# Layer 3's attention with a new order of heads, value products in four column groups, row sums by matmuls with ones, and the division behind the product

## The chip, the cores and the metric

The kernel runs on one core of one Trainium2 chip. The metric is the device time of one execution, in microseconds (us). TensorE (PE) multiplies, VectorE (DVE), ScalarE (ACT) and GpSimd (POOL) work elementwise, SyncE (SP) issues DMAs. "PEld" in the profile is TensorE loading weights, which can lie beside its matmuls.

## What is computed

The program is a chain of four layers; the change is in the last, a cross-attention in which four query heads share a key and value head. Cut to what matters:

```python
B, L, S, H, NH, KVH, HD, GROUPS = 8, 100, 361, 512, 32, 8, 16, 4
q = hidden @ Wq + bq;  k = enc @ Wk + bk;  v = enc @ Wv + bv      # hidden (8,100,512), enc (8,361,512)
q = q.reshape(b, l, KVH, GROUPS, HD).transpose(0, 2, 3, 1, 4)      # k, v: (b, KVH, s, HD)
scores = einsum('bkgld,bksd->bkgls', q, k) / sqrt(HD) + mask
attn = softmax(scores, axis=-1)
out = einsum('bkgls,bksd->bkgld', attn, v).transpose(0, 3, 1, 2, 4).reshape(b, l, H)
x = layernorm(out @ Wo + bo + hidden) * gamma + beta
```

So there are 8 batches of 32 heads, 256 heads in all, each with 100 queries against 361 keys (padded to 363 = 3 x 121).

## The kernel before

`layer3` runs three phases: `layer3_queries`, `layer3_attention` and `layer3_output`. Only the second changes, and with it the order in which the third loads the rows of Wo.

Work goes head by head, and the order on each engine is written out by hand. TensorE takes a "step" for each head h: `scores` (L2252) multiplies the queries of head h with the keys of its pair (96 rows, 364 columns, in the one-pass float32 format) into one of two PSUM banks; `turn` (L2259) transposes the probabilities of head h-4 in three pieces of 121 keys; `attend` (L2272) makes, on three of every four steps, one float32 product of values and turned probabilities of one key and value head. The four heads g of a value head lie side by side in 400 columns; three products (one for each piece j of 121 keys) run over the keys. The output has 32 rows, since the values of an even head fill rows 0 to 15 and those of an odd head rows 16 to 31, with zeros in the other half, so that the two heads of a pair m accumulate in one bank, which is one of two. From step 16 of each batch on, the keys of the next batch (L2230, four products) and its values (L2239, twelve) are projected, a product or four at the end of a step.

VectorE adds the mask, negates and takes the row minimum in one custom instruction (L2402, followed by a read of the accumulator), which frees the bank of the scores; then it inverts the row sum of head h-2 (L2396) and scales that head's probabilities in place (L2407). At the end of a pair it copies four blocks of the product to `attT` (L2385). ScalarE takes the exponential with the row sum beside it (L2326, with a read of the accumulator), and copies the turned probabilities out of PSUM to `probsT` (L2333). GpSimd adds the two parts of the context of the next batch but one (L2202) and spreads the queries over heads (L2211, twelve instructions a batch), once `scored` tells that the scores of the batch two back are done.

TensorE's scores of head h wait for `shifted` of h-2 (two banks), its transposes for `scaled` and for `turned_copied` of two heads back, its value products for `turned_copied` of the fourth head. The lines:

```python
for step in range(H3 + (TAIL if last else 0)):
    if step < H3: scores(step)
    if step - TURN < H3 and not (first and step < TURN): turn(step - TURN)
    v, j = divmod(step - ATTEND - Q3 + 1, Q3)
    if j < NT3 and not (first and v < 0): attend(v, j)
```

## Time and profile before

| what | us |
|---|---|
| median of 3 runs | 4331.4 |
| lowest and highest run | 4328.82, 4335.36 |
| span of the profiled execution | 4338.2 |
| of it, the layer 3 attention from its first scores to its last copy (3736.5 to 4278.6) | 542.1 |
| busy in the whole span: PE, DVE, ACT, POOL | 3694.2, 1757.5, 1221.5, 559.9 |

The profile is of one execution, with a span 6.8 us above the median. A row of the timeline gives start, length, engine, line, operation, output and inputs, the shape and the number of instructions merged; in brackets stands how long the engine had been idle and what ended it. The length of a matmul is its own latency, and matmuls overlap: what one costs in a row of them is the distance from its start to the next start. A float32 product is recorded as two matmuls (x2). The granted clock ("PEclk") is the share of 2.4 GHz; 0.50 is 1.2 GHz.

### The profile page before, as it was taken

How to read it: one execution, taken by the hardware profiler on the slowest of the kernel's cores; microseconds unless marked ns; L12 is line 12 of the kernel's file. 1: busy time of each engine (PE TensorE's matmuls, PEld its weight loads, DVE VectorE, ACT ScalarE, POOL GpSimd, SP SyncE). 2: the span in 40 equal slices, each digit the busy share in tenths (PEclk: the TensorE clock that was granted, in tenths of full speed). 3: DMA queues.
4: the chain of work that ended last, by engine and by line, in shares of the span. 5: the costliest groups of instructions: out<-in, count | busy, mean ns of one | idle time of the engine just before them, and what ended most of it. 6: DMA issues, size and time to landing. Idle time of an engine off the chain costs nothing. (4 is left out here: it accounts for less than half of the span.)

```text
span 4338.2 us, 51209 instructions
## 1 busy us (share of the span) xinstructions
PE 3694.2 (85%) x17671; PEld 2781.4 (64%) x17671; DVE 1757.5 (41%) x3586; ACT 1221.5 (28%) x3084; POOL 559.9 (13%) x475
## 2 busy tenths in 40 slices
PE   4999979796658699999989789898989979688886
PEld 3777758453324487887878578787878867344442
DVE  2445442318873423323232422323232241566664
ACT  2344332111011123222222222222222232445452
POOL 0000020123430300000000100000000010432312
PEclk9999989899979799999999899999999989768688
DMA  2110120100000312222121132222122120110001
GB/s 85 48 46 25 37 77 15 38 10 3 0 10 29 106 42 78 74 59 80 41 73 46 38 109 55 84 55 84 41 78 55 27 80 10 61 38 27 31 2 31
DMA packets 142038, 209.09 MB, mean 48 GB/s; under 512 B 18915, under 2 KB 104357, under 8 KB 141933
## 3 DMA queue, kind: packets, MB, share of 16 engines
q0 software_dynamic: 67584, 94.64, 8.5%
q1 hardware_dynamic: 74348, 113.17, 8.5%
q8 instruction: 51, 0.84, 0.1%
q14 instruction: 55, 0.44, 0.0%
HBM read 191.04 MB, written 13.47 MB: 47 GB/s over the span
## 5 line engine op out<-in xcount | busy, mean ns | idle before, releaser
L63 PE MATMUL work<-cT_layer_hi,wk_layer_hi 128*128 128x362 f32 x1024 | 390.3, 381 | 0.0
L1908 ACT ACTIVATE p_layer<-scores,neg_max_layer 100x362 f32<-100x362 f32 x256 | 144.5, 565 | 740.4 <-DVE neg_max_layer L1963 739.1
L1944 DVE TENSOR_TENSOR values_layer<-work,value_bias_layer 121x512 f32<-121x512 f32 x192 | 132.4, 690 | 519.3 <-PE work L65 519.3
L64 PE MATMUL work<-cT_layer_lo,wk_layer_hi 128*128 128x362 f32 x1024 | 336.8, 329 | 0.0
L65 PE MATMUL work<-cT_layer_hi,wk_layer_lo 128*128 128x362 f32 x1024 | 336.6, 329 | 0.0
L63 PE MATMUL work<-wv_layer_hi,cT_layer_hi 128*121 128x512 f32 x768 | 311.9, 406 | 0.0
L64 PE MATMUL work<-wv_layer_lo,cT_layer_hi 128*121 128x512 f32 x768 | 303.1, 395 | 0.0
L65 PE MATMUL work<-wv_layer_hi,cT_layer_lo 128*121 128x512 f32 x768 | 302.6, 394 | 0.0
L1751 POOL DMA_DIRECT2D cT_layer_hi<-ctxT_hi x64 | 47.7, 745 | 1745.5 <-PE work L65 1743.3
L1890 ACT ACTIVATE keysT_layer<-work 128x361 f32<-128x361 f32 x256 | 120.7, 472 | 510.4 <-PE work L65 510.4
L1820 PE MATMUL o<-pT_layer,values_layer 121*128 121x100 f32 x1536 | 215.8, 276 | 56.9 <-ACT pT_layer L1914 56.9
L1820 PEld LDWEIGHTS o<-pT_layer,values_layer 121*128 121x128 f32 x1536 | 205.4, 191 | 87.5 <-ACT pT_layer L1914 70.2
L2272 PE MATMUL att<-probsT,values 121*32 121x400 f32 x384 | 217.9, 659 | 43.8 <-ACT probsT L2333 43.8
L1963 DVE TENSOR_REDUCE neg_max_layer<-scores 100x1 f32<-100x362 f32 x256 | 136.3, 532 | 220.5 <-PE scores L1802 220.4
L2326 ACT ACTIVATE probs<-probs,neg_max 100x363 f32<-100x363 f32 x256 | 152.6, 596 | 248.0 <-DVE neg_max L2402 246.9
L63 PEld LDWEIGHTS work<-cT_layer_hi,wk_layer_hi 128*128 128x128 f32 x1024 | 193.9, 189 | 29.1
L64 PEld LDWEIGHTS work<-cT_layer_lo,wk_layer_hi 128*128 128x128 f32 x1024 | 194.3, 190 | 24.3
L2402 DVE CUSTOM_DVE_ANT_0 probs<-scores,mask 100x363 f32<-100x363 f32 x256 | 134.8, 527 | 172.5 <-PE scores L2252 171.2
L1802 PE MATMUL scores<-keysT_layer,qT_layer 128*100 128x362 f32 x512 | 198.7, 469 | 0.0
L65 PEld LDWEIGHTS work<-cT_layer_hi,wk_layer_lo 128*128 128x128 f32 x1024 | 193.5, 189 | 0.0
L63 PE MATMUL work<-l_hT_hi,wq_layer_hi 128*128 x256 | 101.8, 398 | 97.1 <-DVE qT_layer L1955 54.6
L2211 POOL TENSOR_TENSOR q_heads<-q_batch,head_rows 32x800 fp32r<-32x800 f32 x96 | 146.0, 1521 | 279.6 <-PE scores L2252 272.2
(353 smaller groups left out, 7737.9 us busy)
## 6 DMA issues: line engine op xcount, KB each, us to landing
cT_layer_hi<-ctxT_hi POOLq DMA_DIRECT2D x64, 722.0 KB, 4.9
cT_layer_lo<-ctxT_lo POOLq DMA_DIRECT2D x64, 722.0 KB, 6.1
l0mlp_staged<-in_L_xattn_mlp_w_dram SPq DMA_DIRECT2D x16, 512.0 KB, 4.2
staged_layer<-in_L_xattn_wq_dram SPq DMA_DIRECT2D x8, 1024.0 KB, 5.2
staged_layer<-in_L_xattn_wk_dram SPq DMA_DIRECT2D x8, 1024.0 KB, 5.1
staged_layer<-in_L_xattn_wv_dram SPq DMA_DIRECT2D x8, 1024.0 KB, 5.1
staged_layer<-in_L_xattn_wo_dram SPq DMA_DIRECT2D x8, 1024.0 KB, 5.6
l2mlp_staged<-in_L_xattn_w_fc_dram SPq DMA_DIRECT2D x16, 512.0 KB, 4.1
```

Of the source, the lines that this page charges most:

```text
L63: pe.matmul(out, cut_a(a.hi), cut_b(b.hi), start=start, stop=False)
L64: pe.matmul(out, cut_a(a.hi), cut_b(b.lo), start=False, stop=False)
L65: return pe.matmul(out, cut_a(a.lo), cut_b(b.hi), start=False, stop=stop)
L1802: pe.matmul(ps_scores[x % 2][0:L, 0:KEYS2], qT[:, j, c * L:(c + 1) * L], keysT[c % 2][:, j, :], start=True, stop=True).then_inc(scored, 1)
L1820: mm = pe.matmul(ps_o[:, j * L:(j + 1) * L], values[c % 2][:, n, j * P:(j + 1) * P], probsT[x % 2][:, n, :], start=(n == 0), stop=(n == NT ...
L1908: act.activation(probs[x % 4][:, 0:KEYS2], ps_scores[x % 2][0:L, 0:KEYS2], ACT.Exp, bias=neg_max[:, x:x + 1], accum_out=sums[:, x:x + 1]). ...
L1944: dve.tensor_tensor(values[c % 2][:, j, :], bank("v", c, j)[0:T2, :], value_bias[:, min(j, 1), :], ALU.add).then_inc(dve_copied, 1)
L1963: dve.tensor_reduce(neg_max[:, x:x + 1], ps_scores[x % 2][0:L, 0:KEYS2], AX.X, ALU.max, negate=True).then_inc(maxed, 1)
L2211: pool.tensor_tensor(q_heads[s][R * block_:R * (block_ + 1), 2 * m:2 * m + 2], q_batch[s][rows, part].unsqueeze(1).broadcast_to([R, 2, Q3, ...
L2272: mm = pe.matmul(ps_att[m % 2][0:R, 0:Q3 * L], values[slot(s, v)][:, j, m, e, :], probsT[v % 2][:, j, :], start=(e == 0 and j == 0), stop= ...
L2326: act.activation(probs[h % PROBS][:], probs[h % PROBS][:], ACT.Exp, bias=neg_max[:, h:h + 1], scale=-1.0, accum_out=sums[:, h:h + 1]).then ...
L2402: dve.tensor_tensor_reduce(probs[h % PROBS][:], ps_scores[h % 2][0:L, 0:N3], mask_add[s][:], -1.0, 3e38, ALU.add, ALU.min, neg_max[:, h:h + 1]
```

## The change

- The heads of a batch are taken in another order (`head_of`): first the 16 heads of the four even value heads (e = 0, pairs m = 0 to 3, four heads g each), then the 16 of the odd ones.
- Turned probabilities of 16 heads are kept (`probsT` has two sets of four tiles). The value products of such a group stand together in three steps, j = 0, 1, 2, of 16: in each, four products for the pairs m, whose outputs are the rows 32m to 32m+31 of one PSUM bank, and behind them four products of the same probabilities with a constant `ones` (1 in the 16 columns of parity e), which write the row sums, 16 times over, in the same places of a second bank.
- The exponential has no accumulator any more; the inverse and the scaling for each head go. Once a batch, VectorE inverts the sums (128x400) and multiplies the product with them into `attT` (128x4x100), in place of 16 small copies.
- The copies of the turned probabilities are shared: ScalarE takes even heads, VectorE odd ones. The transposes now stand 3 steps behind the scores, not 4.
- Loops are written out in full; the four `memset`s of `ones` and other semaphores come with it. Rows of Wo are loaded in eight DMAs as before, in the order that fits the new `attT`.

```diff
-    SCALE, TURN, ATTEND = 2, 4, 5
-    TAIL = ATTEND + NT3 - 1 + 1
-    NEXT = 16
+    GROUP = PAIRS * Q3
+    HEADS = B * H3
+    TURN = 3
+    BURST = GROUP + TURN + 1
+    NEXT = GROUP
+
+    def head_of(h):
+
+        b, x = divmod(h, H3)
+        e, x = divmod(x, GROUP)
+        m, g = divmod(x, Q3)
+        return b, e, m, g
...
+        ones = sb("ones3", [T3, 2, R])
...
-        probsT = [sb(f"probsT3_{i}", [T3, NT3, Q3 * L]) for i in range(2)]
+        probsT = [[sb(f"probsT3_{i}_{m}", [T3, NT3, Q3 * L]) for m in range(PAIRS)] for i in range(2)]
...
-        ps_att = psum_banks(nc, own, "att3_", 2)
+        ps_att, ps_sums = psum_banks(nc, own, "att3_", 2)
...
+            def turn(h):
+                pe.wait_ge(exped, h + 1)
+                if h >= 2:
+                    wait_probsT(pe, h - 2)
...
+            def attend(group, j):
+                b, e = divmod(group, 2)
+                if j == 0:
+                    wait_probsT(pe, GROUP * group + GROUP - 1)
+                    if e == 0:
+                        pe.wait_ge(values_copied, b + 1)
+                        if b:
+                            pe.wait_ge(att_copied, b)
+                for m in range(PAIRS):
+                    pe.matmul(ps_att[R * m:R * (m + 1), 0:Q3 * L], values[b % 2][:, j, m, e, :], probsT[group % 2][m][:, j, :],
+                              start=(e == 0 and j == 0), stop=(e == 1 and j == NT3 - 1))
+                for m in range(PAIRS):
+                    mm = pe.matmul(ps_sums[R * m:R * (m + 1), 0:Q3 * L], ones[:, e, :], probsT[group % 2][m][:, j, :],
                                    start=(e == 0 and j == 0), stop=(e == 1 and j == NT3 - 1))
...
-                        act.activation(probs[h % PROBS][:], probs[h % PROBS][:], ACT.Exp, bias=neg_max[:, h:h + 1],
-                                       scale=-1.0, accum_out=sums[:, h:h + 1]).then_inc(exped, 1)
...
+                    act.activation(probs[h % PROBS][:], probs[h % PROBS][:], ACT.Exp, bias=neg_max[:, h % H3:h % H3 + 1],
+                                   scale=-1.0).then_inc(exped, 1)
+                x = h - TURN
+                if x >= 0 and x % 2 == 0:
+                    act.wait_ge(turned, x + 1)
+                    if x >= 2 * GROUP:
+                        act.wait_ge(attended, x // GROUP - 1)
+                    act.activation(probsT_of(x), ps_turned[x % 2][0:T3, 0:NT3 * L].rearrange("p (j l) -> p j l", j=NT3),
+                                   ACT.Copy).then_inc(copied_act, 1)
...
+            def copy_attended(b):
+                dve.wait_ge(attended, 2 * (b + 1))
+                dve.reciprocal(inverse[:], ps_sums[:, 0:Q3 * L]).then_inc(inverted, 1)
+                dve.wait_ge(inverted, b + 1)
+                dve.tensor_tensor(attT[:, :, b * L:(b + 1) * L], ps_att[:, 0:Q3 * L].rearrange("p (g l) -> p g l", g=Q3),
+                                  inverse[:].rearrange("p (g l) -> p g l", g=Q3), ALU.mult).then_inc(att_copied, 1)
...
+                y = h - TURN
+                if 0 <= y < HEADS and y % 2 == 1:
+                    dve.wait_ge(turned, y + 1)
+                    if y >= 2 * GROUP:
+                        dve.wait_ge(attended, y // GROUP - 1)
+                    dve.tensor_copy(probsT_of(y), ps_turned[y % 2][0:T3, 0:NT3 * L].rearrange("p (j l) -> p j l", j=NT3)
+                                    ).then_inc(copied_dve, 1)
...
-            rows_of = ins["L3_xattn_Wo"].rearrange("(m e g d) n -> g e d m n", m=KT, e=2, g=Q3)
-            for g in range(Q3):
+            rows_of = ins["L3_xattn_Wo"].rearrange("(m e g d) n -> m e d g n", m=KT, e=2, g=Q3)
+            for m in range(KT):
                 for e in range(2):
```


On TensorE, around the first projected values of the next batch, before (names: `att` the product's bank, `work` the projection's):

```order
3197 L2259 MATMUL turned_1<-ident,probs_7 121x100 x3
3198 L2230 MATMUL work_0<-cT_1,Wk 128x363
3199 L2252 MATMUL scores_0<-keys_0,q_heads_0 100x364
3200 L2259 MATMUL turned_0<-ident,probs_0 121x100 x3
3201 L2272 MATMUL att_1<-probsT_1,values_0 32x400
3202 L2239 MATMUL work_1<-Wv,cT_1 121x128 x4
3203 L2252 MATMUL scores_1<-keys_0,q_heads_0 100x364
3204 L2259 MATMUL turned_1<-ident,probs_1 121x100 x3
3205 L2272 MATMUL att_1<-probsT_1,values_0 32x400
```

And the same place now:

```order
3190 L2223 MATMUL work_0<-cT_1,Wk 128x363
3191 L2244 MATMUL scores_0<-keys_0,q_heads_0 100x364
3192 L2252 MATMUL turned_1<-ident,probs_1 121x100 x3
3193 L2265 MATMUL att_0<-probsT_0_0,values_0 32x400
3194 L2265 MATMUL att_0<-probsT_0_1,values_0 32x400
3195 L2265 MATMUL att_0<-probsT_0_2,values_0 32x400
3196 L2265 MATMUL att_0<-probsT_0_3,values_0 32x400
3197 L2268 MATMUL att_1<-probsT_0_0,ones 32x400
3198 L2268 MATMUL att_1<-probsT_0_1,ones 32x400
3199 L2268 MATMUL att_1<-probsT_0_2,ones 32x400
3200 L2268 MATMUL att_1<-probsT_0_3,ones 32x400
3201 L2231 MATMUL work_1<-Wv,cT_1 121x128 x4
```

One product a step has become eight in this step and in the two behind it, and none in the thirteen that follow, where only scores and transposes alternate.

On VectorE, at the end of a batch, before (`ISA` is the custom instruction and its accumulator):

```order
1591 L2396 RECIPROCAL inverse<-sums 100x1
1592 L2402 ISA probs_7,neg_max<-scores_1,mask_0 100x363
1593 L2402 ISA neg_max 100x1
1594 L2407 TENSOR_SCALAR probs_5<-probs_5,inverse 100x363
1595 L2385 TENSOR_SCALAR attT<-att_0 32x100 x4
1596 L2396 RECIPROCAL inverse<-sums 100x1
1597 L2402 ISA probs_0,neg_max<-scores_0,mask_1 100x363
```

And now, behind the last value products of a batch:

```order
864 L2378 ISA probs_6,neg_max<-scores_0,mask_1 100x363
865 L2378 ISA neg_max 100x1
866 L2385 COPY probsT_0_0<-turned_1 121x3x100
867 L2378 ISA probs_7,neg_max<-scores_1,mask_1 100x363
868 L2378 ISA neg_max 100x1
869 L2362 RECIPROCAL inverse<-att_1 128x400
870 L2364 TENSOR_TENSOR attT<-att_0,inverse 128x4x100
871 L2378 ISA probs_0,neg_max<-scores_0,mask_1 100x363
```

For each head, an inverse and a scaling have made room for half a copy; the large inverse and the product with it stand once a batch between two heads' scores.

## Rows read from the trace of the kernel before

**Rows 1.** Windows of the stage and stretches: time, busy per engine, clock, DMA, GB/s.

```profile
3736.50:4278.60 542.10, 461.18 (x1632) 235.18 (x1632) 354.77 (x1225) 287.02 (x840) 159.39 (x97) 0.76 0.07 23
4220.00:4268.00 48.00, 40.82 (x181) 20.54 (x180) 33.37 (x145) 31.42 (x96) 0.00 (x0) 1.00 0.00 1
3930.00:3936.00 6.00, 3.25 (x15) 1.69 (x15) 5.68 (x21) 5.88 (x17) 0.00 (x0) 1.00 0.00 0
4032.00:4048.00 16.00, 15.60 (x38) 7.00 (x37) 6.46 (x29) 6.86 (x21) 0.00 (x0) 0.50 0.00 1
```

**Rows 2.** Groups of instructions, within the attention stage: busy, mean ns, idle before.

```profile
L2272 PE MATMUL att<-probsT,values 121*32 121x400 f32 x384 | 217.9, 659 | 43.8 <-ACT probsT L2333 43.8
...
L2407 DVE TENSOR_SCALAR probs<-probs,inverse 100x363 f32<-100x363 f32 x256 | 167.5, 654 | 0.1
...
L2319 ACT ACTIVATE keys<-keysT 32x363 fp32r<-32x363 f32 x29 | 14.6, 502 | 0.3
```

**Rows 3.** Timeline of PE at the full clock: start, length, instruction.

```profile
4237.80 0.46 PE L2259 MATMUL turned<-ident,probs 100*121 100x100 f32 x3
...
4238.19 0.86 PE L2272 MATMUL att<-probsT,values 121*32 121x400 f32 x2
...
4238.98 0.41 PE L2252 MATMUL scores<-keys,q_heads 96*100 96x364 f32 x1
...
4239.22 0.46 PE L2259 MATMUL turned<-ident,probs 100*121 100x100 f32 x3
...
4239.47 0.39 PE L2252 MATMUL scores<-keys,q_heads 96*100 96x364 f32 x1
...
4275.35 2.20 PE L2272 MATMUL att<-probsT,values 121*32 121x400 f32 x6 [0.51 <-ACT probsT L2333]
```

**Rows 4.** Timeline of PE at half the clock.

```profile
4004.18 0.62 PE L2252 MATMUL scores<-keys,q_heads 96*100 96x364 f32 x1
4004.60 0.78 PE L2259 MATMUL turned<-ident,probs 100*121 100x100 f32 x3
4005.31 1.54 PE L2272 MATMUL att<-probsT,values 121*32 121x400 f32 x2
4006.78 0.62 PE L2252 MATMUL scores<-keys,q_heads 96*100 96x364 f32 x1
4007.20 0.78 PE L2259 MATMUL turned<-ident,probs 100*121 100x100 f32 x3
4007.68 0.61 PE L2252 MATMUL scores<-keys,q_heads 96*100 96x364 f32 x1
```

**Rows 5.** Timeline of DVE and ACT behind the scores of 4238.98.

```profile
4239.60 0.54 DVE L2402 CUSTOM_DVE_ANT_0 probs<-scores,mask 100x363 f32<-100x363 f32 x1 [0.49 <-PE scores L2252]
...
4240.18 0.60 ACT L2326 ACTIVATE probs<-probs,neg_max 100x363 f32<-100x363 f32 x1 [0.43 <-DVE neg_max L2402]
...
4240.78 0.40 ACT L2333 ACTIVATE probsT<-turned 121x300 f32<-121x300 f32 x1
```

**Rows 6.** Timeline of DVE: the scaling while POOL runs.

```profile
3948.63 1.15 DVE L2407 TENSOR_SCALAR probs<-probs,inverse 100x363 f32<-100x363 f32 x1
```

**Rows 7.** Groups of DVE elsewhere in the program: shapes of 128x400.

```profile
L1465 DVE RECIPROCAL y_square<-own_key 128x400 f32<-128x400 f32 x8 | 21.2, 2646 | 2.5 <-ACT own_key L1428 2.5
...
L1467 DVE TENSOR_TENSOR yT<-yT,y_square 128x400 f32<-128x400 f32 x8 | 4.6, 574 | 0.3
...
L2058 DVE COPY xT<-l3q_ps 128x400 f32<-128x400 f32 x4 | 2.3, 574 | 3.2 <-PE l3q_ps L585 3.2
```

**Rows 8.** Timeline of PE: steps with a key product, with a block of value products.

```profile
3917.01 0.46 PE L2259 MATMUL turned<-ident,probs 100*121 100x100 f32 x3
...
3918.12 0.46 PE L2259 MATMUL turned<-ident,probs 100*121 100x100 f32 x3
...
3922.14 1.14 PE L2239 MATMUL work<-Wv,cT 128*121 128x128 f32 x8
...
3923.03 0.41 PE L2252 MATMUL scores<-keys,q_heads 96*100 96x364 f32 x1
```

More of the change, by code:

```diff
@@ L2217, in _, with project_keys @@
         @block.tensor
         def _(pe):
-            pe.sem_inc(projected, 4)
-            for done in (scored, turned):
-                pe.sem_inc(done, 2 * H3)
-            pe.sem_inc(attended, 2 * KV3)
             pe.wait_ge(loaded, 48)
-            def project_keys(b, s, t):
+            def project_keys(b, t):
                 if t == 0:
-                    pe.wait_ge(cT_summed, at(b, 1, 0))
-                    pe.wait_ge(keys_copied, at(b, 1, 0, back=1))
-                mm = pe.matmul(work[0][:, 0:N3], Wk[:, t, :], cT[s][:, t, :], start=(t == 0), stop=(t == KT - 1))
+                    pe.wait_ge(cT_summed, b + 1)
+                    if b:
+                        pe.wait_ge(keys_copied, b)
+                mm = pe.matmul(work[0][:, 0:N3], Wk[:, t, :], cT[b % 2][:, t, :], start=(t == 0), stop=(t == KT - 1))
@@ L2231, in project_keys, with project_values @@
                 if t == KT - 1:
[L2232 to L2237 removed]
+                    mm.then_inc(keys_done, 1)
+            def project_values(b, j):
+                if j == 0 and b:
+                    pe.wait_ge(values_copied, b)
                 for t in range(KT):
[L2239 removed]
+                    mm = pe.matmul(work[1][0:T3, j * P:(j + 1) * P], cT[b % 2][:, t, j * T3:(j + 1) * T3], Wv[:, t, :],
@@ new lines, in project_values, with scores @@
+                    mm.then_inc(values_done, 1)
+            def scores(h):
+                b, e, m, g = head_of(h)
+                if g == 0 and e == 0:
+                    pe.wait_ge(hi_stacked, PAIRS * b + m + 1)
+                    pe.wait_ge(lo_stacked, PAIRS * b + m + 1)
+                    pe.wait_ge(headed, BLOCKS * (PAIRS * b + m + 1))
+                if h >= 2:
+                    pe.wait_ge(shifted, h - 1)
+                pe.matmul(ps_scores[h % 2][0:L, 0:EVEN], q_heads[b % 2][:, 2 * m + e, g, :], keys[b % 2][:, m, :],
+                          start=True, stop=True).then_inc(scored, 1)
@@ L2291, in _ @@
             for t in range(KT):
-                project_keys(0, 0, t)
+                project_keys(0, t)
             for j in range(NT3):
-                project_values(0, 0, j)
-            batches(pe, steps)
+                project_values(0, j)
+            for h in range(HEADS - GROUP + BURST + NT3):
+                if h < HEADS:
+                    scores(h)
+                if 0 <= h - TURN < HEADS:
+                    turn(h - TURN)
+                group, j = divmod(h - BURST, GROUP)
+                if group >= 0 and j < NT3:
+                    attend(group, j)
+                b, x = divmod(h, H3)
+                if b + 1 < B:
+                    if 0 <= x - NEXT < KT:
+                        project_keys(b + 1, x - NEXT)
+                    if 0 <= x - NEXT - KT < NT3:
+                        project_values(b + 1, x - NEXT - KT)
@@ L2346, in _ @@
             for m in range(PAIRS):
-                stack_pair(0, 0, m)
-            batches(act, steps)
+                stack_pair(0, m)
+            for h in range(HEADS + TURN):
+                if h < HEADS:
+                    act.wait_ge(shifted, h + 1)
+                    act.activation(probs[h % PROBS][:], probs[h % PROBS][:], ACT.Exp, bias=neg_max[:, h % H3:h % H3 + 1],
[7 more added lines that the diff above has]
+                                   ACT.Copy).then_inc(copied_act, 1)
+                b, x = divmod(h, H3)
+                if b + 1 < B:
+                    if x == NEXT + KT:
+                        copy_keys(b + 1)
+                    if x == NEXT + KT + 1:
+                        round_keys(b + 1)
+                    if 0 <= x - NEXT - KT - 2 < PAIRS:
+                        stack_pair(b + 1, x - NEXT - KT - 2)
         @block.vector
```

280 lines of the change are left out of this document (96 added, 184 removed).

## The prediction

> **What bounds the kernel now.** The windows come first [rows 1]: the attention of layer 3 takes 542.1 us, PE is busy for 461 of them, DVE for 355, ACT for 287, and PE's granted clock is 0.76 on average. So PE leads, but it runs at two speeds and has gaps. 8 batches in 542.1 us are 67.8 us each. Of the two levels, the clock is at 0.50 for (1 - 0.76) / 0.5 = 48% of the time. Then the timeline of PE, read by distances from start to start. At the full clock [rows 3] transposes take 0.25 us up to the next scores (4239.22 to 4239.47), scores 0.24 (4238.98 to 4239.22), and a product of the values 0.79 (4238.19 to 4238.98), while the transposes ahead of it need 0.39 in place of 0.25. The product of 32 output rows is two records; in six of them in a row (2.20 us, one being 0.52) the starts stand 0.335 apart. So of 0.79 + 0.39 us, 0.67 is product and some 0.26 is spent on entering and leaving it. A step with a product is 1.43 us, one without 0.50 for PE. At half the clock [rows 4] the same are 2.60 (4004.18 to 4006.78) and 0.90 (4006.78 to 4007.68). The next view is what goes on behind the scores [rows 5]: DVE starts 0.62 us after them, the exponential 0.58 later, the copy 0.60 later and takes 0.40. Where POOL spreads the queries, the scaling takes 1.15 us [rows 6] where the mean over all is 0.654 [rows 2]; then DVE is behind and PE waits. In the last batch POOL has nothing to do, and the clock is 1.00 with PE busy for 40.8 of 48 us [rows 1]. In 3930 to 3936 PE was busy for only 3.25 of 6 us, and the half clock came behind it; in 4032 to 4048 it stayed at 0.50 with PE busy for 15.6 of 16.
>
> By these prices a batch all at the full clock would be 24 x 1.43 and 8 x about 1.6 (the fourth step waits for its copy) and 5 for projections and 3 for stacking, 55 us; all at half the clock some 83. The 67.8 found lie 45% of the way: call this the **slow share** of the work.
>
> **Part by part, for one batch.** In the new order a batch has 32 steps: 6 burst steps with eight float32 products each, 4 with a key product, 22 plain.
>
> Plain steps. PE needs 0.50 at the full clock and 0.90 at half [rows 3, 4]. ACT has an exponential (0.51 apart from its accumulator read, by 0.60 for both) and half a copy of 0.40 in steady flow, some 0.7 us; DVE 0.54 and half a copy, whose price I take from the copy of 128x400, 0.574 [rows 7], so 0.75 to 0.8. The loop through all engines is longer: scores to DVE 0.62, to the exponential 0.58, to the copy 0.60, its 0.40, then transposes 0.25, which is 2.45 us for three steps [rows 3, 5], or 0.82 with a little for signals 0.84. I take 0.84 at the full clock and 0.90 at half: 22 of them are 18.5 or 19.8 us. Before, the row sum's read, the inverse and the scaling were in this loop; they go, and with them the collision with POOL.
>
> Key steps: 1.11 (3917.01 to 3918.12) [rows 8], at half 0.90 + 2 x 0.61 = 2.11: four are 4.4 or 8.4 us. Value projections are three times 0.89 (3922.14 to 3923.03), 2.7 or 5.3 us; they now stand in burst steps. Neither is new.
>
> Bursts. Each of the six has scores 0.25, transposes 0.39 and 0.12 to leave the narrow form (at half 0.42, 0.71, 0.14) [rows 3, 4], and eight products. A product is 0.67 us alone [rows 3]. No row has products in different column groups, so the price needs bounds. Serial: 8 x 0.67 = 5.34 us. All four column groups at once: 2 x 0.67 = 1.33. In between lies what the two records of a product suggest: the second goes to the same columns as the first and must follow it, but the first of the next product goes to other columns and could run beside the second; with starts in program order, every two records cost one distance, 8 x 0.333 + 0.333 = 3.0 us. I take 3.0: it needs no reordering, only independent columns, and it lies between the ends. That gives 3.76 us a step at the full clock and 7.27 at half, 22.6 or 43.6 us a batch. Nothing covers this: with two banks of scores, ACT and DVE are done within a microsecond and wait, so burst time adds to plain time.
>
> The Trainium skill ("TensorE: Matmul & The Clock Gate", Part 3) states that matmuls of 32 columns in three column groups gained 2.38 times, with a span of about one matmul and 4 ns for each further one. An estimate from that figure, four groups in the span of little more than one, puts eight products nearer 1.33 than 3.0 us and the time nearer the rival A below. No trace here shows it.
>
> Stacking the keys: three plain steps carry two ACT copies of 0.50 [rows 2] on top of 0.7, so 3 x (1.7 - 0.84) = 2.6 us. End of a batch: the inverse over 128x400 is 2.65 and the product with it 0.57 [rows 7], 3.2 us of DVE between two heads' scores; some 0.7 is slack, so 2.5 us in which PE runs dry, against four copies a pair before.
>
> Sum of a batch: full clock 18.5 + 4.4 + 2.7 + 22.6 + 2.6 + 2.5 = 53.3 us; half clock 19.8 + 8.4 + 5.3 + 43.6 + 2.4 + 2.4 = 81.9. At the full clock that is hardly less than today's 55: in my case the products are as dear per head as before (6 x 3.0 = 18 us against 24 x 0.67 = 16), since the sums by matmuls double them. What is saved is DVE's and ACT's share, and through it the clock. The collision with POOL, which led into half-clock stretches, is gone; new are plain stretches in which PE streams for only 0.50 of 0.84 us, and 2.5 us dry once a batch. I take a slow share of 0.35, somewhat under today's 0.45: 53.3 + 0.35 x 28.6 = 63.3 us, times 8 is 506, 36 us less than 542.1. The output's loads are eight as before, the start of the stage is bound by POOL's first queries and ACT's keys as before, and the memsets of the ones lie before a wait for the context: nothing for these, if POOL's 12 instructions of 1.5 us keep ahead of the new order, which wants the last pair at head 12 rather than 24; a batch of 60 us leaves room. The profiled span 4338.2 becomes 4302, and with the median 6.8 us below the span, **4295 us**.
>
> **Rivals.**
>
> A, column groups fully parallel: burst steps of 2.09 (3.94) us, 12.5 (23.6) a batch; a batch 43.2 (61.9), at 0.35 slow 49.7, in all 398 us, 144 less: 4187. For it: the groups share no columns. Against it: two records of one product use the same columns and stand next to each other.
>
> B, the forecast. At the full clock throughout it gives 426, so 4215; at a slow share of 0.6, 564, so 4353. It turns into a loss from a slow share of 0.51 on.
>
> C, serial, the slower side: products of different column groups do not overlap. Burst steps 6.1 (12.0) us, 36.6 (71.8) a batch; a batch 67.3 (110.1), at 0.35 slow 82.3, in all 658, 116 more: 4447. Even at the full clock it is 538, no gain. From about 3.55 us for eight products on (at a slow share of 0.35) the change is a loss. For it: in all rows before, matmuls of PE stand one behind another.
>
> D, pairs overlap, but the clock is at half nearly throughout: 655 us, 113 more: 4444. For it: the half clock followed a stretch with PE busy for 54% [rows 1]. Against it: by records, scores of 0.39 and transposes of 0.5 fill a plain step, and at half the clock PE is busy all the time.
>
> E, the change comes to nothing net (within 0.2%): the gain of the short loop is given back in bursts.
>
> **How the numbers follow.** A 0.17, B 0.44, C 0.26, D 0.08, E 0.05. Two runs of this kernel can be told apart from about 0.2%, 8.7 us. Faster: A, 0.82 of B and a little of C, 0.55; same 0.08; slower 0.37. The range must hold 8 in 10: below 4170 lies a part of A, above 4440 more than half of C and of D, together about 0.2. B's own range is 4215 to 4353.
>
> **What would show it.** In the profile after: eight products of a burst step, from the first product's start to the next scores' start: 1.4, 3.1 or 5.5 us at the full clock decide between A, B and C. Plain steps should be 0.8 to 0.9 us apart in either clock. The clock of the stage should be above 0.76, and DVE's copies of 300 columns near 0.45. DVE's inverse of 2.65 us should stand once a batch with PE idle behind it. The forecast is wrong if the records of a product do not pair as I think, or if the clock follows the plain steps down.

## The result, and the profile after

The changed kernel takes **4187.7 us** (median of 4 runs, 4181.44 to 4189.84), the kernel before 4330.4 (4 runs, 4328.82 to 4335.36): a ratio of 0.967, 95% interval 0.965 to 0.969, 143 us faster. The forecast was 4295 us, 36 us faster. The time lay inside the range and is that of rival A (4187). That the two agree to the microsecond is partly luck: rival A put the stage at 398 us and it took 392.4; against that it put the median 6.8 us below the profiled span, and the span, now 4184.7, lies 3.0 below the median.

The attention stage, first scores to last copy. Columns: window, its length, then busy time and instructions of PE, PEld, DVE, ACT and POOL, granted clock, DMA share, GB/s:

```profile
3733.90:4126.30 392.40, 339.02 (x2016) 238.70 (x2016) 236.13 (x729) 222.66 (x456) 159.23 (x97) 0.76 0.10 32
```

Against the first of [rows 1] the stage is 149.7 us shorter: 49.05 us a batch in place of 67.8. (The medians differ by less, 143, since the span before lay above its median and the one now lies below.) PE is busy for 122 us less though it runs 384 records more; DVE for 119 less, ACT for 64 less. The mean clock is the same 0.76.

The groups of instructions of the stage (busy us, mean ns of one | idle time before them in us, what ended it):

```profile
L2244 PE MATMUL scores<-keys,q_heads 96*100 96x364 f32 x256 | 139.2, 545 | 30.5 <-DVE neg_max L2378 27.8 <-ACT keys L2309 2.5
...
L2385 DVE COPY probsT<-turned 121x300 f32<-121x300 f32 x128 | 60.0, 468 | 3.3 <-PE turned L2252 1.8
...
L2265 PE MATMUL att<-probsT,values 121*32 121x400 f32 x384 | 49.2, 588 | 0.7 <-DVE probsT L2385 0.7
L2268 PE MATMUL att<-probsT,ones 121*32 121x400 f32 x384 | 46.2, 555 | 0.0
...
L2362 DVE RECIPROCAL inverse<-att 128x400 f32<-128x400 f32 x8 | 21.2, 2653 | 6.1 <-PE att L2268 6.1
...
L2364 DVE TENSOR_TENSOR attT<-att,inverse 128x400 f32<-128x400 f32 x8 | 4.6, 574 | 0.3
```

The 384 records of value products were 217.9 us of busy time [rows 2]. Now 384 of values and 384 of sums are 95.4 together, though one record is hardly shorter (588 and 555 ns against 659): they overlap. The inverse takes 2653 ns and the product 574, as the shapes in [rows 7] let expect.

The timeline of PE through the last burst step of a group (3983.67 to 3985.80) and into the plain steps behind it, to set beside [rows 3] (lines left out are marked):

```profile
3983.67 0.41 PE L2244 MATMUL scores<-keys,q_heads 96*100 96x364 f32 x1
3983.92 0.46 PE L2252 MATMUL turned<-ident,probs 100*121 100x100 f32 x3
3984.32 0.88 PE L2265 MATMUL att<-probsT,values 121*32 121x400 f32 x8
3985.01 0.85 PE L2268 MATMUL att<-probsT,ones 121*32 121x400 f32 x8
3985.80 0.41 PE L2244 MATMUL scores<-keys,q_heads 96*100 96x364 f32 x1
...
3986.84 0.41 PE L2244 MATMUL scores<-keys,q_heads 96*100 96x364 f32 x1
3987.82 0.53 PE L2252 MATMUL turned<-ident,probs 100*121 100x100 f32 x3 [0.58 <-ACT probs L2318]
3990.47 0.41 PE L2244 MATMUL scores<-keys,q_heads 96*100 96x364 f32 x1 [2.12 <-DVE neg_max L2378]
3990.95 0.78 PE L2252 MATMUL turned<-ident,probs 100*121 100x100 f32 x3
3991.43 0.60 PE L2244 MATMUL scores<-keys,q_heads 96*100 96x364 f32 x1
...
3993.77 0.61 PE L2244 MATMUL scores<-keys,q_heads 96*100 96x364 f32 x1
...
3994.64 0.60 PE L2244 MATMUL scores<-keys,q_heads 96*100 96x364 f32 x1
```

Four value products take 0.69 us (3984.32 to 3985.01), four sums with the way out of the narrow form 0.79, eight products in all **1.48 us** up to the next scores, where the forecast had 3.1 and rival A 1.4. The step is 2.13. Behind the burst stands the inverse on DVE, and PE is idle for 2.12 us before the scores of 3990.47:

```profile
3986.70 2.65 DVE L2362 RECIPROCAL inverse<-att 128x400 f32<-128x400 f32 x1
```

From the transposes of 3990.95 on lengths are those of half the clock (0.78 and 0.60, as in [rows 4]), and plain steps follow each other at 0.87 (3993.77 to 3994.64).

Within another burst at the full clock one can look at slices of a few hundredths of a microsecond, here with the value products alone (columns: window, length, PE and PEld with their records, clock, DMA share, GB/s; a record counts in every slice that it touches, and its end is modelled):

```profile
3905.88:3905.92 0.04, 0.02 (x4) 0.02 (x4) 1.00 0.00 0
3905.92:3905.96 0.04, 0.04 (x4) 0.04 (x8) 1.00 0.00 0
...
3906.20:3906.24 0.04, 0.04 (x4) 0.00 (x0) 1.00 0.00 0
3906.24:3906.28 0.04, 0.04 (x8) 0.00 (x0) 1.00 0.00 0
```

This burst begins at 3905.90. Four records have started by 3905.92. The next four join between 3906.24 and 3906.28, some 0.36 later, and all eight weights are loaded by 3906.06. Read with the runs on one and two groups below, in which one and two records start at once, the first four are the first records of the four pairs: a record waits for the one before it in its own columns, and not for the one before it in the program.

The starts of the scores, from which each step's length follows, give this table (mean of batches 1 to 6, in us; "clock" is what most of these steps had). Burst and value projection stand in one step in steps 20 to 22; the 2.7 us of the projections are the prediction's price, which the run with the projections moved bears out below (0.9 us a step).

| steps of a batch | after | clock | forecast, full / half clock |
|---|---|---|---|
| bursts (4 to 6, 20 to 22) without projections | 14.8 | half in step 4, else mostly full | 22.6 / 43.6 |
| key steps (16 to 19) | 6.3 | half, full from 18 or 19 on | 4.4 / 8.4 |
| value projections, in steps 20 to 22 | 2.7 | full | 2.7 / 5.3 |
| the other 22, with stacking and inverse | 25.1 | half throughout in 11 to 14 | 23.6 / 24.6 |
| batch | 48.9 | | 53.3 / 81.9 |

Step 9, which holds the inverse, is 3.63; steps 25 to 27, in which the keys are stacked, are 1.93, 1.52 and 1.58; step 4 is 3.71, steps 5 and 6 are 2.41 and 2.12. Before, the same mean of a batch was 70.0.

### The profile page after: what moved, and what is told of

It reads as the page before. It is cut to its first block and busy times, and to the rows that moved or that the text cites. A ratio compares the mean times of both kernels' runs of the same rounds, so it can differ in the third digit from the quotient of the medians.

```text
span 4184.7 us, 50251 instructions
## 1 busy us (share of the span) xinstructions
PE 3566.8 (85%) x18055; PEld 2780.5 (66%) x18055; DVE 1639.4 (39%) x3090; ACT 1156.1 (28%) x2700; POOL 559.9 (13%) x479
## 5 line engine op out<-in xcount | busy, mean ns | idle before, releaser
L2252 PEld LDWEIGHTS turned<-ident,probs 100*121 100x121 f32 x768 | 159.9, 258 | 46.1 <-ACT probs L2318 31.1
L2252 PE MATMUL turned<-ident,probs 100*121 100x100 f32 x768 | 168.6, 344 | 21.4 <-ACT probs L2318 19.5
```

The costliest lines, as they stand in the source:

```text
L2252: mm = pe.transpose(ps_turned[h % 2][0:T3, j * L:(j + 1) * L], probs[h % PROBS][:, j * T3:(j + 1) * T3], k.ident[0:L, 0:L])
```

## The experiments

The theory is that the four column groups run fully beside each other, each from a queue of its own, and that this is where the forecast lost its 108 us. There are three rivals: the products are cheap for another reason (the clock, the order of the heads); the gain comes from the shorter loop of DVE and ACT; the overlap is bought by the order in which the products are issued.

The runs were made in groups. The kernel before ran in each, with medians of 4317 to 4333 us. The changed kernel ran in two, with 4187.7 and 4187.3, and its attention stage took 392.4 us in both traces. Differences below are between medians, those to the changed kernel across groups but for the last three runs; the stages in the traces give the same differences to within 5 us, so one of 4 to 6 us is no more than a hint.

**One and two column groups.** All products go to rows 0 to 31 of their bank, or by turns to two groups (`R * (m % 2)` in place of `R * 0`), the sums likewise; all else stays. The products of several pairs are thereby added into one place, so that part of the result is mixed up. The flags that begin and end a sum are adapted, and two `memset`s fill the rows that are no longer written.

```diff
-                    pe.matmul(ps_att[R * m:R * (m + 1), 0:Q3 * L], values[b % 2][:, j, m, e, :], probsT[group % 2][m][:, j, :],
+                    pe.matmul(ps_att[R * 0:R * 0 + R, 0:Q3 * L], values[b % 2][:, j, m, e, :], probsT[group % 2][m][:, j, :],
...
```

> The changed kernel, but all four pairs' products and sums go to rows 0 to 31 of their banks, one column group (rows 32 to 127 are filled with ones once; the attention's result is left mixed up). Theory G (products in different column groups run fully beside each other, 1.48 us for eight at the full clock): now eight cost 5.3 us, 3.9 more in 48 burst steps at the full clock and twice that at half; with a third of the work at half, 30 us a batch, some 240 more than the changed kernel: 4430, and in the bursts products start 0.335 us apart. Rival S (the gain is the shorter loop of DVE and ACT, not the column groups): within 20 us of 4188.

> The same with pairs 0 and 2 in column group 0 and pairs 1 and 3 in group 1 (result mixed up). Theory G: eight products 2.7 us, 1.2 more a burst step, with a third at half clock 9.4 us a batch: 4262. If a third or fourth group brings nothing, within 10 us of 4188.

Measured: **4371.4 us** (4368.86 to 4374.26) with one group, ratio to before 1.0085 (1.0057 to 1.0113), and **4253.9** (4251.86 to 4255.98) with two. The burst, with one group:

```profile
3916.28 0.46 PE L2252 MATMUL turned<-ident,probs 100*121 100x100 f32 x3
3916.67 2.87 PE L2265 MATMUL att<-probsT,values 121*32 121x400 f32 x8
3919.38 2.85 PE L2268 MATMUL att<-probsT,ones 121*32 121x400 f32 x8
3922.16 1.14 PE L2231 MATMUL work<-Wv,cT 128*121 128x128 f32 x8
```

and with two:

```profile
3908.59 1.54 PE L2265 MATMUL att<-probsT,values 121*32 121x400 f32 x8
3909.96 1.51 PE L2268 MATMUL att<-probsT,ones 121*32 121x400 f32 x8
3911.40 0.41 PE L2244 MATMUL scores<-keys,q_heads 96*100 96x364 f32 x1
```

Eight products take 5.49, 2.81 and 1.48 us with one, two and four groups: 16 records x 0.335 divided by the number of groups, and some 0.13 for leaving the form. 48 bursts x 4.01 are 192 us, x 1.33 are 64; measured were +184 and +66. This is the whole effect: the time of a burst's products goes with one over the number of groups. The order of the heads is the same in all three kernels, and so is the clock in the bursts shown, so neither explains it. The two expectations (4430 and 4262) priced a third of the work at half the clock and were too high by 59 and 8 us; the bursts ran at the full clock but for the one of step 4. With one group the change as a whole is a loss, by 0.85%: rival C was right on the sign in case of no overlap, and wrong on the size (+116 us expected, +39 found). Its slow share of 0.35 was too high for long bursts: some 16 steps of a batch are at half the clock with one group and with four, and nearly all of them are short ones, so the mean clock of 3740 to 4090 is 0.82 against 0.76.

**Another order of issue.** Value product and sum of a pair stand next to each other, so that each following instruction goes to the same column group as the one before it.

```diff
                 for m in range(PAIRS):
                     pe.matmul(ps_att[R * m:R * (m + 1), 0:Q3 * L], values[b % 2][:, j, m, e, :], probsT[group % 2][m][:, j, :],
                               start=(e == 0 and j == 0), stop=(e == 1 and j == NT3 - 1))
-                for m in range(PAIRS):
                     mm = pe.matmul(ps_sums[R * m:R * (m + 1), 0:Q3 * L], ones[:, e, :], probsT[group % 2][m][:, j, :],
```

> The changed kernel with the products and sums of a burst in another order: value product and sum of one pair next to each other, so that four records in a row go to the same column group. Theory G with a queue for each column group: no difference, 4188 within 8. Rival Q (records start in program order, and those of the changed kernel overlap only because other groups come soon): only the last record of a pair overlaps the first of the next, 13 of 16 distances of 0.335, 4.3 us for eight products, some 180 more: 4365.

Measured: **4193.9 us** (4190.98 to 4195.21), 6 above the changed kernel and 171 below the time for starts in program order. The timeline:

```profile
3908.43 0.90 PE L2265 MATMUL att<-probsT,values 121*32 121x400 f32 x8
3909.13 0.87 PE L2267 MATMUL att<-probsT,ones 121*32 121x400 f32 x8
3909.93 1.13 PE L2231 MATMUL work<-Wv,cT 128*121 128x128 f32 x8
```

In the program the first sum is the second instruction of the eight. In the trace all eight value records have started before it does, at 3909.13, as if the order of issue had not been changed. The Trainium skill ("TensorE: Matmul & The Clock Gate", Part 3) says of tiled matmuls that they are monotone in start, in the order of the program, with no reordering. These rows do not agree: starts go by column group. The Trainium skill's speedup of 2.38 for three column groups, which the prediction cited and left out of its sum, fits what was found: here it is 5.49 / 1.48 = 3.7 for four.

**Without the sums.** The four products with ones are left out (the sums' bank holds ones all through), so the result is not divided.

```diff
-                for m in range(PAIRS):
-                    mm = pe.matmul(ps_sums[R * m:R * (m + 1), 0:Q3 * L], ones[:, e, :], probsT[group % 2][m][:, j, :],
-                                   start=(e == 0 and j == 0), stop=(e == 1 and j == NT3 - 1))
```

> The changed kernel without the products with ones (the sums are left out; the inverse is taken of ones). Their price: 0.69 us in 48 burst steps at the full clock, twice that at half, 5.4 us a batch with a third at half: 43 less, 4145. Rival: the sums lie in time in which TensorE would wait for VectorE anyway: no difference.

Measured: **4167.9 us** (4161.27 to 4170.31), 20 us less where 43 were expected. The burst itself came out as expected, 0.81 us in place of 1.48:

```profile
3998.74 0.88 PE L2265 MATMUL att<-probsT,values 121*32 121x400 f32 x8
3999.55 1.13 PE L2231 MATMUL work<-Wv,cT 128*121 128x128 f32 x8
```

But the mean record of a value product grew from 588 to 685 ns and the mean clock of 3740 to 4090 fell from 0.76 to 0.67: with shorter bursts more of their steps lie at half the clock (steps 5 and 6 at 2.56 and 2.19 us, no shorter than the 2.41 and 2.12 with the sums). So the sums, which last 48 x 0.67 = 32 us, cost 20.

**The kernel before, with the short loop only.** No row sum beside the exponential, no inverse, no scaling; all else is as before. The division is left out.

```diff
-                    pe.wait_ge(scaled, at(b, H3, h))
+                    pe.wait_ge(exped, at(b, H3, h))
...
-                                       scale=-1.0, accum_out=sums[:, h:h + 1]).then_inc(exped, 1)
+                                       scale=-1.0).then_inc(exped, 1)
...
-                        dve.reciprocal(inverse[:, x % H3:x % H3 + 1], sums[:, x % H3:x % H3 + 1]).then_inc(inverted, 1)
...
-                        dve.tensor_scalar(probs[x % PROBS][:], probs[x % PROBS][:], inverse[:, x % H3:x % H3 + 1], None, ALU.mult
-                                          ).then_inc(scaled, 1)
```

> The kernel before, with its own order and its float32 products one at a time, but without the row sum at the exponential, without the inverse and without the scaling; the probabilities are left undivided, that part of the computation is left out. It shows what the shorter loop through DVE and ACT is worth without column groups. My working: TensorE needs 24 x 1.43 + 8 x 0.50 at the full clock and some 7 us for projections and stacking, 45 to 50 us a batch, about 80 at half. Theory 'the column groups carry the gain': TensorE was the bound, so the batch falls from 67.8 only to 56 to 63 us and the time lies at 4235 to 4295. Theory 'the short loop carries the gain, and the groups only keep it': at or below 4190.

Measured: **4262.5 us** (4252.48 to 4267.71), ratio 0.9869 (0.9848 to 0.989), 55 us under the kernel before, which took 4317.2 beside it, and inside the 4235 to 4295 of the theory that the groups matter. Its stage:

```profile
3736.86:4205.00 468.14, 397.35 (x1632) 207.80 (x1632) 193.32 (x713) 263.07 (x584) 159.25 (x97) 0.89 0.08 27
```

So 55 us of the gain need no column groups (68 against the 4330.4 of the first group of runs), and 75 us more separate this kernel from the changed one, in medians (4262.5 to 4187.7) as in stages (468.1 to 392.4). (By the traces the stage fell by 74 against the kernel before, but the span traced there, 4338.2, is above all its medians.) DVE has fallen from 355 to 193 us, PE's clock has risen to 0.89, and PE is busy for 397 of 468 us; the batch is 58.5 us.

**The changed kernel, with the scaling put back.** DVE multiplies each head's probabilities by 1.0 between exponential and transposes, which stand a step later.

```diff
-    TURN = 3
+    TURN = 4
...
-                pe.wait_ge(exped, h + 1)
+                pe.wait_ge(scaled, h + 1)
...
+                z = h - 2
+                if 0 <= z < HEADS:
+                    dve.wait_ge(exped, z + 1)
+                    dve.tensor_scalar(probs[z % PROBS][:], probs[z % PROBS][:], 1.0, None, ALU.mult).then_inc(scaled, 1)
```

> The changed kernel, with an additional scaling of each head's probabilities by 1.0 on DVE between exponential and transposes, and the transposes four steps behind the scores; nothing is left out. It puts the length of the loop and the DVE work back without touching the products. DVE gets 0.41 us more a step, 1.15 where POOL spreads the queries (about 12 to 14 of 32 steps). If the short loop is worth what I think, a step becomes about 1.1 and beside POOL 1.85 us, +10 to +16 us a batch: 4270 to 4310. If the loop had slack, under +15: below 4203.

Measured: **4235.7 us** (4232.97 to 4239.22), +48 where +82 to +122 was expected. Here DVE runs while POOL works:

```profile
3956.09 0.52 DVE L2379 CUSTOM_DVE_ANT_0 probs<-scores,mask 100x363 f32<-100x363 f32 x1
3956.54 0.08 DVE L2379 DVE_READ_ACCUMULATOR2_ANT neg_max<- 100x1 f32 x1
3956.54 1.21 DVE L2384 TENSOR_SCALAR probs<-probs 100x363 f32<-100x363 f32 x1
3957.67 0.46 DVE L2390 COPY probsT<-turned 121x300 f32<-121x300 f32 x1
```

The collision of [rows 6] is there again (1.21), and it hits the scaling alone: the custom instruction and the copy, which read PSUM, keep 0.52 and 0.46. A batch is 5.5 us longer than the changed kernel's (54.4 against 48.9), and the steps, each set against the one before it in the changed kernel, tell where: 3.8 in steps 0 to 5, where POOL works, and 1.6 in steps 10 to 12, where DVE has the inverse and POOL its last addition; in the rest, the bursts of steps 21 to 23 among them, the scaling costs next to nothing. Only 9 or 10 scalings of a batch (1 to 6) were slowed, where 12 to 14 were assumed. So nearly all that the scaling costs stands where it collides with POOL. It is only one part of what the run before took out, so that the 48 us and the 55 us are near each other without measuring the same thing.

**The inverse in four pieces, one after the other.**

```diff
-                dve.reciprocal(inverse[:], ps_sums[:, 0:Q3 * L]).then_inc(inverted, 1)
+                cols = slice(g * L, (g + 1) * L)
+                dve.reciprocal(inverse[:, cols], ps_sums[:, cols]).then_inc(inverted, 1)
...
-                if group >= 0 and group % 2 == 1 and j == NT3:
-                    copy_attended(group // 2)
+                if group >= 0 and group % 2 == 1 and NT3 <= j < NT3 + Q3:
+                    copy_attended(group // 2, j - NT3)
```

> The changed kernel, with the inverse and the product behind it cut into four pieces of 100 columns, one in each of four steps, in place of one inverse of 2.65 us and one product of 0.57. If the dry spell behind the inverse costs what I put it at (2.5 us a batch), most of it goes: -12 to -20 us, 4168 to 4176. If PE's dry time there is hidden in the whole, or the pieces push the following heads as much as the one piece: within 4 us of 4188. If the clock also falls because of the dry spell: more than -20.

Measured: **4181.2 us** (4177.95 to 4186.34), 6 less; hardly anything, and between the two expectations. One of the four steps on DVE:

```profile
3984.05 0.52 DVE L2381 CUSTOM_DVE_ANT_0 probs<-scores,mask 100x363 f32<-100x363 f32 x1
3984.50 0.08 DVE L2381 DVE_READ_ACCUMULATOR2_ANT neg_max<- 100x1 f32 x1
3984.50 0.47 DVE L2388 COPY probsT<-turned 121x300 f32<-121x300 f32 x1
3984.88 0.77 DVE L2364 RECIPROCAL inverse<-att 128x100 f32<-128x100 f32 x1
3985.68 0.26 DVE L2366 TENSOR_TENSOR attT<-att,inverse 128x100 f32<-128x100 f32 x1
3985.86 0.52 DVE L2381 CUSTOM_DVE_ANT_0 probs<-scores,mask 100x363 f32<-100x363 f32 x1
```

DVE is full from one head to the next (3984.05 to 3985.86). Steps 9 to 13 became 1.44, 1.82, 1.54, 1.72 and 1.58 us, 8.1 in all, out of 3.63, 0.96, 1.46, 0.88 and 0.88, which were 7.8. Cutting the block did not create slack; the dry spell only changed its shape. What was gained stands in steps 15 to 18 (5.0 us in place of 6.3), where the clock was back at full earlier.

**All copies on ACT.**

```diff
-                if x >= 0 and x % 2 == 0:
+                if x >= 0:
                     act.wait_ge(turned, x + 1)
...
-                    dve.tensor_copy(probsT_of(y), ps_turned[y % 2][0:T3, 0:NT3 * L].rearrange("p (j l) -> p j l", j=NT3)
-                                    ).then_inc(copied_dve, 1)
```

> The changed kernel, with all copies of the turned probabilities on ACT and none on DVE. ACT then needs 0.51 + 0.40 = 0.91 us a step in plain steps (the loop was 0.84) and 1.4 in steps that stack keys; DVE only 0.54. Expected +1.5 to +3.5 us a batch, 4200 to 4216, if ACT becomes the bound of the plain steps as the sum says; if DVE (0.54 + 0.24, plus the inverse) was what set the steps, it gains: 4165 to 4185.

Measured: **4197.3 us** (4196.16 to 4198.7), +10, just under the expected 4200 to 4216. ACT's copies go from 51.4 to 103.1 us. The plain steps have room for them: most are 0.88 us by PE's half clock, and exponential and copy follow each other on ACT at 0.81 from start to start (3994.41 to 3995.22 in this trace), where the sum had 0.91. The 0.7 us by which a batch is longer stand in steps 25 to 29, where ACT stacks the keys besides (8.4 us in place of 7.7). Sharing the copies is worth 10 us by the medians, 7 by the stages.

**Projections moved, scores doubled, and the inverse spread.** These ran with the changed kernel beside them on the same chip. First the changed kernel:

> The changed kernel once more, unaltered, on the chip on which the three kernels that follow run, as what they are compared with. Expected: 4188 within 10 us.

It took **4187.3 us** (4184.46 to 4190.5). Next, the value projections stand five steps later:

```diff
+    LATE = 5
...
-                    if 0 <= x - NEXT - KT < NT3:
-                        project_values(b + 1, x - NEXT - KT)
+                    if 0 <= x - NEXT - KT - LATE < NT3:
+                        project_values(b + 1, x - NEXT - KT - LATE)
...
-                    if x == NEXT + KT + NT3:
+                    if x == NEXT + KT + LATE + NT3:
```

> The changed kernel, with the three value projections of the next batch moved out of the burst steps 20 to 22 into steps 25 to 27, in which TensorE waits for DVE and ACT while these stack the keys. Nothing is left out. In the trace of after those burst steps last 3.21, 3.01 and 3.01 us against 2.12 without a projection, and steps 25 to 27 last 1.93, 1.52 and 1.58 with TensorE busy for 0.94, 0.94 and 0.81. Theory 'the projections lie uncovered in the burst steps and would be covered in the thin ones': -2.5 us a batch for 7 batches, -14 to -19 against after. If they hold up the transposes in the new place as well: 0 to -6. Theory 'the thin steps 25 to 28 let the clock fall': the clock then stays at 1.00 through steps 27 to 31, another -2 to -10.

Measured: **4173.8 us** (4171.8 to 4181.67), 13 less, just short of the expected 14 to 19. Steps 20 to 22 fell to 2.32, 2.12 and 2.12; steps 25 to 27 rose from 5.03 to 5.80 us in sum, so they were not quite free. The stretch of steps 25 to 27 and the one behind it up to the next batch's step 4, first of the changed kernel:

```profile
4013.37:4018.30 4.93, 2.60 (x14) 1.61 (x13) 4.72 (x17) 4.79 (x10) 0.00 (x0) 1.00 0.00 0
4018.30:4026.57 8.27, 7.85 (x35) 6.94 (x34) 6.30 (x22) 6.95 (x15) 3.75 (x3) 0.51 0.07 17
```

then with the projections there:

```profile
4000.65:4006.45 5.80, 4.53 (x38) 4.08 (x37) 5.03 (x14) 5.62 (x12) 0.00 (x0) 1.00 0.00 0
4006.45:4013.95 7.50, 5.84 (x35) 4.54 (x34) 6.21 (x26) 5.91 (x14) 4.13 (x3) 0.87 0.07 19
```

With PE busy for 2.60 of 4.93 us the clock fell to half right behind; with 4.53 of 5.80 it stayed at 1.00 for four to seven steps more. That made the second stretch 0.77 us shorter, nearly what the projections cost in the first (0.87); but the clock was at half again before the burst of step 4 (3.87 us).

The next kernel multiplies the scores of every step without value products twice:

```diff
+                if not NT3 > (h - BURST) % GROUP:
+                    pe.matmul(ps_scores[h % 2][0:L, 0:EVEN], q_heads[b % 2][:, 2 * m + e, g, :], keys[b % 2][:, m, :],
+                              start=True, stop=True)
                 pe.matmul(ps_scores[h % 2][0:L, 0:EVEN], q_heads[b % 2][:, 2 * m + e, g, :], keys[b % 2][:, m, :],
```

> The changed kernel, with the scores of every step that has no value products multiplied twice into the same bank; the result is the same, the work is 0.24 us more a step at the full clock and 0.40 at half. Theory 'the clock falls since the plain steps keep TensorE busy for only 0.50 of 0.88 us': it holds the full clock more often, the mean clock of the attention rises from 0.76 to over 0.85, and the time stays within -15 to +10 us of after. Theory 'it falls behind the stalls of steps 9 and 25 to 28, whatever the plain steps hold': the clock stays near 0.76, each of the 13 to 16 plain steps a batch at half the clock becomes 1.3 in place of 0.88 us, +5 to +6 us a batch, +35 to +50.

Measured: **4210.2 us** (4205.55 to 4212.7), +23. The clock did not rise:

```profile
3734.00:4133.00 399.00, 363.88 (x2158) 275.61 (x2159) 236.96 (x721) 222.05 (x451) 159.49 (x97) 0.76 0.10 32
```

Denser plain steps did not hold the clock: it fell in step 10 or 11, behind the stall of step 9, and in step 27, much as in the changed kernel (9 to 11, and 27 or 28). Steps at half the clock became 1.18 us; the second scores cost 0.30 there and not 0.40, and bursts began earlier at the full clock (step 4 at 3.33), hence +23 and not +35 to +50.

The last kernel has r2's edit and, besides, pieces of the inverse two steps apart, with ACT taking the copies meanwhile:

```diff
+    def on_act(h):
+        return h % 2 == 0 or h >= H3 and 4 <= h % H3 < 12
...
-                if x >= 0 and x % 2 == 0:
+                if x >= 0 and on_act(x):
...
-                if 0 <= y < HEADS and y % 2 == 1:
+                if 0 <= y < HEADS and not on_act(y):
...
-                if group >= 0 and group % 2 == 1 and j == NT3:
-                    copy_attended(group // 2)
+                if group >= 0 and group % 2 == 1:
+                    if j in (3, 5, 7, 9):
+                        invert(group // 2, (3, 5, 7, 9).index(j))
+                    if j == 10:
+                        copy_attended(group // 2)
```

> The changed kernel with both stalls of TensorE in a batch attacked, nothing left out: the inverse in four pieces of 100 columns in steps 7, 9, 11 and 13 and one product in step 14, while ACT takes over DVE's copies of heads 4 to 11; and the value projections in steps 25 to 27. Cutting the inverse alone gained nothing, since the four pieces in a row made four steps of 1.4 to 1.8 us out of one of 3.6: DVE was full. Here DVE has 0.54 + 0.39 a step, ACT 0.91. Expected: step 9 from 3.63 to about 1.0, the rest of 7 to 14 at 0.88 to 1.0, -2 us a batch; with the values -4.5 us a batch, -30 to -36 against after, 4152 to 4158. If the clock then also stays up into the next burst (steps 4 and 5 at 2.1 each in place of 3.71 and 2.42), another -15: 4137 to 4143. If ACT becomes the bound of steps 7 to 14 or the clock falls all the same with no gain behind it: 4165 to 4180.

Measured: **4153.8 us** (4150.77 to 4159.85), ratio to before 0.9612 (0.9585 to 0.9639), 33 us under the changed kernel and the fastest of all. The same place on DVE, behind a burst:

```profile
3969.52 0.78 DVE L2369 RECIPROCAL inverse<-att 128x100 f32<-128x100 f32 x1
3970.21 0.47 DVE L2387 CUSTOM_DVE_ANT_0 probs<-scores,mask 100x363 f32<-100x363 f32 x1
3970.61 0.08 DVE L2387 DVE_READ_ACCUMULATOR2_ANT neg_max<- 100x1 f32 x1
3970.92 0.54 DVE L2387 CUSTOM_DVE_ANT_0 probs<-scores,mask 100x363 f32<-100x363 f32 x1 [0.23 <-PE scores L2249]
3971.38 0.08 DVE L2387 DVE_READ_ACCUMULATOR2_ANT neg_max<- 100x1 f32 x1
3971.38 0.78 DVE L2369 RECIPROCAL inverse<-att 128x100 f32<-128x100 f32 x1
```

Two heads to one piece, and DVE has idle time again. Steps 9 to 15 sum to 7.2 us in place of 9.8; the batch is 44.4 us, 4.5 less than 48.9, the expected amount. In every second batch steps 11 to 13 ran at the full clock, 0.80 us each, where the prediction gave a plain step 0.84. The clock in front of step 4 was at half all the same (step 4 at 3.93), so the further 15 us did not come.

## Why the prediction was wrong

**The direction and the mechanisms of the plain steps were right, the price of a burst was not.** Of the 14.2 us between the 63.3 us a batch of the forecast and the 49.05 found, all stands in one term: bursts were put at 22.6 + 0.35 x 21.0 = 30.0 us and took 14.8, and the other terms together came out 1 us above the forecast. That is in part luck: at the slow share of 0.35 these others were 24.0 (found 25.1), 5.8 for the key steps (6.3) and 3.6 for the projections (2.7), and the misses partly cancel.

- *The eight products, at 3.0 us and 0.12 to leave: the failed step.* At the full clock 1.48 us were found for both. The argument was that a second record must follow the first in its columns, which is so (0.34 to 0.36 apart), and that starts go "in program order", so that a blocked second record holds up the next pair. The slices of the burst and the run with the other order of issue show that it does not hold it up. Then only 4 records x 0.335 stand behind each other in a column group, the lower bound of 1.33. The three times (5.49, 2.81, 1.48 us with one, two and four groups) bear it out. The term was put between the bounds on an argument that no row supported; the lower bound, with its own chance of 0.17, was the case that came.
- *Bursts at half the clock.* 43.6 us were the larger part of the half-clock sum, and so the clock seemed to be worth 28.6 us a batch. With short bursts it is 18.7 (rival A's 43.2 and 61.9), and the 49.05 lie 31% of the way, against 0.35 assumed. So the slow share was nearly right, if for another distribution of the clock than the one it was argued from.
- *The clock itself.* "Above 0.76" was wrong: 0.76, as before. What changed is where the half clock lies. Before, it lay on steps of 2.4 to 2.6 us that would have been 1.43; now mostly on 11 to 14 plain steps of a batch, which are 0.88 at half the clock and were 0.80 at the full one in the last run. The places where it still costs are step 4 (3.71, where step 20 of the run with the projections moved is 2.32 at the full clock), step 5 (0.3) and the key steps 16 to 18 (1.9 in sum): some 3.6 us a batch, 25 in all (an estimate from these rows).
- *Plain steps, stacking, inverse.* 25.1 us against 23.6 at the full and 24.6 at half the clock. The inverse, forecast at 2.5 us, made step 9 longer than a plain step by 3.63 - 0.88 = 2.75, with DVE's 2.65 us in it, and DVE's copies of 300 columns take 0.468 (0.45 forecast). The key steps, 6.3 us, lie between 4.4 and 8.4.
- *The short loop.* It is worth 55 us in the old order; the scaling alone costs 48 in the new one. The prediction had the loop's gain mostly given back in the bursts, which was so only without column groups: with one group all of it is given back and 39 us more, which is rival C's sign.

So the gain of 143 us is, by the runs: 55 to 68 from the short loop in the old order, and 75 more when the new order with column groups, the sums by matmuls and the shared copies join it. No run has the new order of heads without the bursts, so that its own share is not shown. Inside the changed kernel four groups in place of one are worth 184 us, of which the doubled number of products had to be paid.

What stays open: what lets the clock fall in front of step 4. Filling the stacking steps and spreading the inverse moved the places where it fell by some steps, doubling the scores hardly moved them, and none held it up to the burst.

## What to carry to other kernels

Float32 products with 32 output rows that stood one behind another in the same rows of PSUM took 3.7 times as long here as in the four groups of 32 rows: put independent ones into the four groups and issue them together; in what order hardly matters (6 us of 4188). Before putting a price between two far bounds, ask which mechanism would have to exist for the middle, and whether a row shows it. A stall made by a full engine wasn't removed by cutting the work into pieces; here it was removed by pieces further apart together with other work taken off that engine (the two were not tried singly), and a projection costs least in steps in which TensorE waits anyway.

## What the runs showed of the hardware

- Float32 products in four column groups overlap fully, both records of each: 16 records in 1.48 us with the way out, against 5.49 in one group. At the full clock each group takes its records in its own order, 0.335 us apart, whatever is issued between them.
- An inverse on DVE takes 0.77 us for 100 columns and 2.65 for 400 (128 rows, float32), which by the line through the two is 0.15 us fixed and 6.3 ns a column, an estimate; the product behind it 0.26 and 0.57.
- Beside POOL, DVE's scaling from SBUF to SBUF, 0.34 us alone, mostly rose to 0.84 to 1.22 us and in single cases to 3.0 (the run with the scaling put back), while instructions of DVE that read PSUM kept their 0.46 and 0.52.
- The same clock average (0.76) goes with 67.8 and with 49.05 us a batch; what counts is which steps are at half. The two traces of the changed kernel, from two chips, have the same stage (392.4 us).
